# Three memsets ahead of a stage's gathers, and expert slots aligned so that one transfer brings an expert's rows

## The chip, the cores and the metric

The kernel runs on 1 core of one Trainium2 chip, in a single launch. The metric is the device time of that core in microseconds. The engines are TensorE (PE in the profile, with PEld for its weight loads), VectorE (DVE), ScalarE (ACT), GpSimd (POOL) and SyncE (SP). Each runs its own queue of instructions in order and waits on semaphores for the others. GpSimd issues the indirect transfers (gathers and scatters by row index), SP the plain ones.

## What is computed

One block of a graph network over 2500 nodes of 256 features and 80000 edges, in float32. The last two steps are the ones that matter here:

```python
xn = layernorm(x)
x = x + gatv2(xn, edges) + lambda_mix(xn)      # node sums, elu, layernorm, residual
h = layernorm(x)
probs = softmax(h @ gate_w + gate_b)           # 8 experts, top 1
idx, prb = argmax(probs), max(probs)
pos = running count of tokens of the same expert, minus 1
kept = pos < C                                 # C = ceil(1.25 * 2500 / 8) = 391
buf[idx, pos] = h                              # for kept tokens, else dropped
y = relu(buf @ w1 + b1) @ w2 + b2              # per expert, w1 256 x 1024, w2 1024 x 256
x = x + y[idx, pos] * prb * kept               # with nan and inf replaced
```

## The kernel before

Nodes are held as 20 tiles (`TILES`) of 128 nodes, in 5 groups of four tiles (`FOURS`). The kernel has four stages, each a block with one program per engine and a barrier of all engines at its end: `survey` (first layer norm, tables of edges, projections), `attend` (all edges in 176 quads of 512; it leaves running sums in the DRAM array `d_hist`), `node_update`, and `experts`.

**Node update** (lines 1505 to 1819). GpSimd gathers the finished sums of each tile out of `d_hist` into `acc`, one indirect transfer per tile (L1586, 20 in all); the four of group b count up semaphore `fetched[b]`. Behind these it sets three small buffers: `neghalf`, the zero row of `before`, and the padding columns of `pack` (L1588 to L1590). Then it waits for its own memsets and makes reciprocal roots: `roots(b, "var1", ...)` when DVE has `ve1` of group b, and `roots(b - 1, "var2", ...)` when DVE has `ve2`. At last `dispatch(b)` scatters each tile's packed rows to their slots in the DRAM array `d_in` (L1583).

DVE first waits for the memsets (`init` at 2) and writes one column of `pack` (L1644). Then it goes over the groups in a pipeline of five steps, in this order in each round b: `shifts(b-3)`, `logits(b-4)`, `places(b-5)`, `mean_rows(b)` (waits for `fetched[b]`; divides the sums, adds the bias), `residual(b-2)` (needs the first roots and PE's `mix`; writes `x1`), `hidden(b-1)` (elu, adds xn, statistics, writes `ve1`), `choose(b-4)` (the expert of each token). PE runs `mixes(b)` (from the third group on only when `x1` is far enough, as the banks are reused), `turns_of` (transposes and gate products) and `positions` (L1811, L1812: counts in each expert). ACT does exponentials and the second normalization.

SP waits for all five `fetched` semaphores, then loads the weights of experts 0 and 1 (`load_expert`, L1825 to L1828), then stores `x1` of each group to the output.

**Experts** (lines 1831 to 2009). `d_in` holds 391 slots (`CAP`) for each of 8 experts, one behind the other; a row is 516 words (`PACK`): the normalized features, the token's number plus 1, its weight, and `x1`. The slots are cleared in `survey`. `load_rows(e)` brings an expert's slots as four transfers of 98 rows (`CT`), to 98 partitions; the fourth, which is to hold 97, reads one row over into the next expert. Experts 0 to 3 are loaded at the stage's start, one behind the other, expert e + 2 later from the loop over e. PE turns the rows (L1892), widens (L1903), narrows (L1915) and turns back (L1925); ACT empties the banks; DVE cleans the result; GpSimd scatters it to the output.

The order of work is written out by hand for every engine; there is no planner.

Of the kernel before, what the change touches and what calls it, by code (L numbers as in the profile page):

```python
# [26 lines left out]
TILES = -(-NODES // P)  # L27
# [25 lines left out]
EXPERTS, FF = 8, 1024  # L53
CAP = -(-5 * NODES // (4 * EXPERTS))
FCH = FF // P
CT = -(-CAP // 4)
CTS = [CT, CT, CT, CAP - 3 * CT]
TRASH = EXPERTS * CAP
HEAD_COLS = DIM + 4
PACK = HEAD_COLS + DIM  # L60
ZERO_ROWS = 4
# [1443 lines left out]
def node_update(nc, ctx, m, a):  # L1505
# [6 lines left out]
    fetched = [m.sems.enter_context(nc.semaphore(f"upd_fetched{b}")) for b in range(TILES // 4)]  # L1512
    bias, gamma, gate_w, gate_b = m.bias, m.gamma, m.gate_w, m.gate_b
    FOURS = TILES // 4
    acc = sb("u_acc", [P, TILES, HEADS, HCOLS])
    den = sb("u_den", [P, 2, 4 * HEADS])
    out = sb("u_out", [P, 2, 4, DIM])
# [20 lines left out]
    which = sb("u_which", [P, TILES])  # L1538
# [3 lines left out]
    posr = sb("u_posr", [P, TILES])  # L1542
    dropped = sb("u_dropped", [P, TILES])
    at = sb("u_at", [P, TILES])
# [15 lines left out]
    with nc.Block() as block:  # L1560
# [15 lines left out]
        @block.gpsimd  # L1576
        def _(pool):
            def dispatch(b):
                pool.wait_ge(s["packed"], b + 3)
                pool.wait_ge(s["placed"], b + 1)  # L1580
                pool.wait_ge(s["norm"], 4 * b + 4)
                for n in range(4 * b, 4 * b + 4):
                    pool.indirect_dma_start(m.d_in, bass.IndirectOffsetOnAxis(ap=place_all[:, n:n + 1], axis=0),  # L1583
                                            pack[:, n, :], None, bounds_check=TRASH - 1, oob_is_err=False).then_inc(s["scattered"], 16)
            for n in range(TILES):
                pool.indirect_dma_start(acc[:, n, :, :].rearrange("p h c -> p (h c)"), None, m.d_hist,  # L1586
                                        bass.IndirectOffsetOnAxis(ap=m.final[:, n:n + 1], axis=0)).then_inc(fetched[n // 4], 16)
            pool.memset(neghalf[:, :], -0.5).then_inc(s["init"], 1)  # L1588
            pool.memset(before[:, 0:1, :], 0.0).then_inc(s["init"], 1)
            pool.memset(pack[:, :, DIM + 2:HEAD_COLS], 0.0).then_inc(s["packed"], 1)  # L1590
            pool.wait_ge(s["init"], 2)

            def roots(b, var, ve, rs, done):
                cols = slice(4 * b, 4 * b + 4)
                pool.wait_ge(s[var], b + 1)
                rstd_pool(pool, rs[:, cols], ve[:, cols], neghalf[:, :]).then_inc(s[done], 1)
            for b in range(FOURS):
                roots(b, "var1", ve1, rs1, "rstd1")
                if 1 <= b:
                    roots(b - 1, "var2", ve2, rs2, "rstd2")  # L1600
            dispatch(0)
            roots(FOURS - 1, "var2", ve2, rs2, "rstd2")
            for b in range(1, FOURS):
                dispatch(b)
            pool.wait_ge(s["scattered"], 16 * TILES)
# [35 lines left out]
        def _(dve):  # L1641
# [36 lines left out]
            def places(b):  # L1678

                tiles = slice(4 * b, 4 * b + 4)  # L1680
                dve.wait_ge(s["posps"], b + 1)
                ch.step(dve.tensor_tensor(pos[:, tiles, :], ps_pos[:, 4 * b * EXPERTS:(4 * b + 4) * EXPERTS].rearrange("p (n e) -> p n e", n=4),
                                          hot[:, tiles, :], ALU.mult))
                ch.step(dve.tensor_reduce(posr[:, tiles], pos[:, tiles, :], AX.X, ALU.add))
                dve.tensor_scalar(dropped[:, tiles], posr[:, tiles], float(CAP), float(2 * TRASH), ALU.is_gt, ALU.mult).then_inc(s["gate_chain"], 1)
                dve.scalar_tensor_tensor(out=at[:, tiles], in0=which[:, tiles], scalar=float(CAP), in1=posr[:, tiles],
                                         op0=ALU.mult, op1=ALU.add).then_inc(s["gate_chain"], 1)
                dve.scalar_tensor_tensor(out=pack[:, tiles, DIM + 1], in0=posr[:, tiles], scalar=float(CAP), in1=best[:, tiles],
                                         op0=ALU.is_le, op1=ALU.mult).then_inc(s["packed"], 1)
                ch.n += 2  # L1690
                dve.wait_ge(s["gate_chain"], ch.n)
                dve.scalar_tensor_tensor(out=place_all[:, tiles], in0=dropped[:, tiles], scalar=-1.0, in1=at[:, tiles],
                                         op0=ALU.add, op1=ALU.add).then_inc(s["placed"], 1)
# [137 lines left out]
def experts(nc, ctx, m, a):  # L1831
# [5 lines left out]
    rows = [spare[r // 2][:, r % 2, :, :] for r in range(4)]  # L1837
    landed = [m.sems.enter_context(nc.semaphore(f"exp_rows{r}")) for r in range(4)]
# [8 lines left out]
    out = sb("f_out", [P, 2, 4, DIM])  # L1847
# [3 lines left out]
    with nc.Block() as block:  # L1851
        @block.sync
        def _(sp):
            def load_rows(e):
                if e >= 4:
                    sp.wait_ge(s["out"], (e - 3) * 2)
                for j in range(4):
                    lo = e * CAP + j * CT
                    sp.dma_start(rows[e % 4][0:CT, j, :], m.d_in[lo:lo + CT, :]).then_inc(landed[e % 4], 16)  # L1859
            for e in range(4):  # L1860
                load_rows(e)
            for e in range(2, EXPERTS):
                sp.wait_ge(s["y"], (e - 1) * 2)
                load_expert(sp, m, a, e, e % 2)
                if e + 2 < EXPERTS:
                    load_rows(e + 2)
            for q in range(2):
                sp.wait_ge(s["stored"][q], 64 * (EXPERTS // 2))
# [15 lines left out]
        @block.tensor  # L1884
        def _(pe):
            def turn_rows(e):
                pe.wait_ge(landed[e % 4], (e // 4 + 1) * 64)
                if e >= 1:
                    pe.wait_ge(s["rowsb"], e * 2)
                for half in range(2):  # L1890
                    for j, n in enumerate(CTS):
                        last = pe.transpose(m.bank[half][:, j * CT:j * CT + n], rows[e % 4][0:n, j, half * P:half * P + P], m.ident[0:n, 0:n])  # L1892
                    last.then_inc(s["rowst"], 1)
# [67 lines left out]
        def _(dve):  # L1961
            def tokens(e):

                q = e % 2
                dve.wait_ge(landed[e % 4], (e // 4 + 1) * 64)
                if e >= 2:
                    dve.wait_ge(s["stored"][q], e // 2 * 64)
                ids = rows[e % 4][0:CT, :, DIM]
                dve.tensor_scalar(token[0:CT, q, :], ids, 0.0, float(4 * PAD), ALU.is_equal, ALU.mult).then_inc(s["index"], 1)
                dve.wait_ge(s["index"], 2 * e + 1)  # L1970
                dve.scalar_tensor_tensor(out=index[0:CT, q, :], in0=token[0:CT, q, :], scalar=-1.0, in1=ids,
                                         op0=ALU.add, op1=ALU.add).then_inc(s["index"], 1)
# [82 lines left out]
```

## Time and profile before

| | us |
|---|---|
| median of 3 runs | 1382.27 |
| lowest, highest | 1379.01, 1382.58 |
| profiled execution, whole time | 1380.51 |
| its span in the trace | 1378.8 |
| mean granted TensorE clock | 0.924 of full |

The page says that 1138.9 us of the span have PE busy, 1076.6 DVE, 835.5 ACT and 807.0 GpSimd. By stage: the edges take from about 175 to 1033 us, the node update from there to 1167.5, the experts the rest. The time axis of all rows counts from the start of the span. A "busy" share is only what an engine executes; idle time of an engine costs something only where others wait for what it does next.

### The profile page before, as it was taken

How to read it: one execution, taken by the hardware profiler on the slowest of the kernel's cores; microseconds unless marked ns; L12 is line 12 of the kernel's file. 1: busy time of each engine (PE TensorE's matmuls, PEld its weight loads, DVE VectorE, ACT ScalarE, POOL GpSimd, SP SyncE). 2: the span in 40 equal slices, each digit the busy share in tenths (PEclk: the TensorE clock that was granted, in tenths of full speed). 3: DMA queues.
4: the chain of work that ended last, by engine and by line, in shares of the span. 5: the costliest groups of instructions: out<-in, count | busy, mean ns of one | idle time of the engine just before them, and what ended most of it. 6: DMA issues, size and time to landing. Idle time of an engine off the chain costs nothing. (4 is left out here: it accounts for less than half of the span.)

```text
span 1378.8 us, 24446 instructions
## 1 busy us (share of the span) xinstructions
PE 1138.9 (83%) x5685; PEld 838.5 (61%) x5685; DVE 1076.6 (78%) x2310; ACT 835.5 (61%) x3252; POOL 807.0 (59%) x844
## 2 busy tenths in 40 slices
PE   7969789888889989888888989898773553999994
PEld 4537577666667767666666666677552442565652
DVE  5957889998999999899999999999952883044445
ACT  2421278887878888788888887788851231222220
POOL 5217777777777777777777777777805125013133
PEclk9979999999999999999999999999987665899997
DMA  6576578878788888788888877778414313345420
GB/s 167 200 243 187 167 190 208 209 201 198 200 198 207 208 205 202 195 198 206 207 205 208 204 205 189 204 205 210 122 47 135 95 54 138 112 112 150 124 83 16
DMA packets 162621, 234.91 MB, mean 170 GB/s; under 512 B 40085, under 2 KB 131490, under 8 KB 161747
## 3 DMA queue, kind: packets, MB, share of 16 engines
q1 hardware_dynamic: 118434, 127.66, 33.3%
q0 software_dynamic: 41216, 103.67, 29.8%
q10 hardware_dynamic: 2880, 2.66, 0.6%
q14 instruction: 71, 0.58, 0.1%
q8 instruction: 20, 0.33, 0.1%
HBM read 187.01 MB, written 48.91 MB: 171 GB/s over the span
## 5 line engine op out<-in xcount | busy, mean ns | idle before, releaser
L1456 ACT ACTIVATE e_prod<-gathered_rows,e_prod 128x64 f32<-128x64 f32 x2728 | 670.4, 334 | 5.7
L1010 POOL DMA_INDIRECT gathered_rows<-d_xl,e_idx x576 | 549.4, 954 | 175.5 <-issue 163.3
L1400 PE MATMUL bank<-e_prod,e_selt 128*128 128x260 f32 x1408 | 363.7, 404 | 41.7 <-DVE e_acc L1127 21.3
L1400 PEld LDWEIGHTS bank<-e_prod,e_selt 128*128 128x128 f32 x1408 | 273.2, 199 | 96.1 <-issue 46.9
L1346 PE MATMUL bank<-e_xr,e_sel 128*128 128x256 bf16 x2112 | 294.6, 277 | 1.8 <-DVE e_sel L1080 0.4
L1351 PE MATMUL bank<-gathered_rows,ident 128*128 128x256 f32 x704 | 220.6, 395 | 46.5 <-DMA gathered_rows<-d_xl,e_idx 32.5
L1346 PEld LDWEIGHTS bank<-e_xr,e_sel 128*128 128x128 bf16 x2112 | 206.5, 99 | 73.2 <-issue 9.0
L1105 DVE TENSOR_REDUCE e_score<-e_edge 128x16 f32<-128x1024 f32 x176 | 213.0, 1210 | 0.3
L1010 POOL DMA_INDIRECT gathered_rows<-d_xl,src_cols x128 | 122.7, 958 | 71.3 <-issue 36.1
L1351 PEld LDWEIGHTS bank<-gathered_rows,ident 128*128 128x128 f32 x704 | 108.0, 194 | 69.1 <-DMA gathered_rows<-d_xl,e_idx 49.0
L1881 POOL DMA_INDIRECT out_dram<-f_out,f_index x32 | 44.9, 1404 | 160.8 <-DVE f_out L1996 155.9
L1088 DVE TENSOR_TENSOR e_edge<-bank,gathered_rows 128x512 f32<-128x512 f32 x176 | 119.5, 679 | 10.6 <-PE bank L1351 10.4
L1113 DVE TENSOR_TENSOR e_selt<-bank,cyclic_cols 128x512 f32<-128x512 f32 x176 | 119.9, 681 | 0.0
L1094 DVE SCALAR_TENSOR_TENSOR e_edge<-bank,att_relu 128x512 f32<-128x512 f32 x176 | 119.5, 679 | 0.0
L1098 DVE SCALAR_TENSOR_TENSOR e_edge<-e_edge,bank 128x512 f32<-128x512 f32 x176 | 118.6, 674 | 0.0
L1903 PE MATMUL bank<-f_rowst,w_rows 128*128 128x391 f32 x256 | 88.6, 505 | 0.7 <-ACT f_rowst L1944 0.7
L1915 PE MATMUL bank<-f_hid,w_rows 128*128 128x391 f32 x256 | 85.8, 492 | 0.0
L1445 ACT ACTIVATE e_rr<-e_drop 1x4 f32<-1x4 f32 x22 | 4.5, 204 | 125.8 <-DVE e_drop L1185 110.3
L1127 DVE SCALAR_TENSOR_TENSOR e_acc<-e_acc,keep_cols,bank 128x260 f32<-128x260 f32 x154 | 73.2, 475 | 7.3 <-PE bank L1400 7.2
L1903 PEld LDWEIGHTS bank<-f_rowst,w_rows 128*128 128x128 f32 x256 | 49.7, 195 | 38.1 <-issue 3.8
L1951 ACT ACTIVATE f_hid<-bank,b_cols 128x391 f32<-128x391 f32 x64 | 37.6, 588 | 50.6 <-PE bank L1903 50.6
L1915 PEld LDWEIGHTS bank<-f_hid,w_rows 128*128 128x128 f32 x256 | 47.9, 189 | 33.6
(314 smaller groups left out, 1101.1 us busy)
## 6 DMA issues: line engine op xcount, KB each, us to landing
e_xr<-d_xr SPq DMA_DIRECT2D x176, 192.0 KB
d_hist<-e_acc SPq DMA_DIRECT2D x176, 130.0 KB
e_drow<-d_rel SPq DMA_DIRECT2D x176, 128.0 KB
w_rows<-in_L_ffn_w_dram SPq DMA_DIRECT2D x16, 1024.0 KB, 7.2
gathered_rows<-d_xl,e_idx POOLq DMA_INDIRECT x576
d_in<-zero SPq DMA_DIRECT2D x6, 1032.0 KB, 5.0
e_rows<-d_rows SPq DMA_DIRECT2D x22, 192.5 KB
d_xr<-a_xr SPq DMA_DIRECT2D x20, 192.0 KB, 2.0
```

Of the source, the lines that this page charges most:

```text
L1010: pool.indirect_dma_start(xl[:, q.slot * G + g, :], None, m.d_xl, bass.IndirectOffsetOnAxis(ap=column, axis=0)).then_inc(gathered[q.slot], 16)
L1088: dve.tensor_tensor(edge[:, b, 2:4, :], ps_edge[b][1][:, :].rearrange("p (g c) -> p g c", g=2), xl[:, q.slot * G + 2:q.slot * G + 4, 0:DIM ...
L1094: dve.scalar_tensor_tensor(out=edge[:, b, 0:2, :], in0=ps_edge[b][0][:, :].rearrange("p (g c) -> p g c", g=2), scalar=0.0, in1=m.att_relu[ ...
L1098: dve.scalar_tensor_tensor(out=edge[:, b, 2:4, :], in0=edge[:, b, 2:4, :], scalar=0.0, in1=att_relu.unsqueeze(1).to_broadcast([P, 2, DIM]) ...
L1105: dve.tensor_reduce(score[:, p, :, q.at * G:q.at * G + G].rearrange("p h g -> p g h"), edge[:, b, :, :].rearrange("p g (h c) -> p g h c", ...
L1113: dve.tensor_tensor(selt[:, b, :, :], lane_up.unsqueeze(1).to_broadcast([P, G, P]), m.cyclic[:, bass.ds(q.k * G, G)].unsqueeze(2).to_broad ...
L1346: last = pe.matmul(out, sel[:, b, g * P:g * P + P], xr[:, r, part * DIM:part * DIM + DIM], start=(part == 0), stop=(part == 2 and g >= 2))
L1351: last = pe.matmul(out, m.ident[:, :], xl[:, q.slot * G + g, 0:DIM], start=False, stop=True)
L1400: last = pe.matmul(ps_agg[b], selt[:, b, g, :], flat(prod[:, b, g, :, :]), start=(g == 0), stop=(g == G - 1))
L1456: last = act.activation(prod[:, b, g, h, 0:HEAD], xl[:, q.slot * G + g, h * HEAD:h * HEAD + HEAD], ACT.Copy, scale=prod[:, b, g, h, HEAD:H ...
L1903: last = pe.matmul(m.bank[2 + f % 2][:, 0:CAP], w1[:, q, half, f * P:f * P + P], rowst[:, q, half, :], start=(half == 0), stop=(half == 1))
L1915: last = pe.matmul(m.bank[4 + to][:, 0:CAP], w2[:, q, f, to * P:to * P + P], hid[:, f, :], start=(f == 0), stop=(f == FCH - 1))
```

## The change

`node_update`: the three memsets come first in GpSimd's program. Of the 20 gathers, the twelve of groups 0 to 2 follow them; group 3's four are issued behind `roots(0, "var1", ...)`, group 4's behind `roots(1, "var1", ...)` and `roots(0, "var2", ...)`.

`experts`: each expert's slots begin at a multiple of `SLOTS` = 4 x 98 = 392, so slot 391 of every expert is never written and stays zero. One transfer of 98 partitions x 4 rows x 516 words brings an expert's slots in place of four, and the semaphore `landed` counts 16 per expert in place of 64. `TRASH`, the size of `d_in` and the bound of the scatter, grows from 3128 to 3136.

```diff
--- before.py
+++ after.py
@@ -55,7 +55,8 @@
 FCH = FF // P
 CT = -(-CAP // 4)
 CTS = [CT, CT, CT, CAP - 3 * CT]
-TRASH = EXPERTS * CAP
+SLOTS = 4 * CT
+TRASH = EXPERTS * SLOTS
 HEAD_COLS = DIM + 4
 PACK = HEAD_COLS + DIM
 ZERO_ROWS = 4
@@ -1582,12 +1583,15 @@
                 for n in range(4 * b, 4 * b + 4):
                     pool.indirect_dma_start(m.d_in, bass.IndirectOffsetOnAxis(ap=place_all[:, n:n + 1], axis=0),
                                             pack[:, n, :], None, bounds_check=TRASH - 1, oob_is_err=False).then_inc(s["scattered"], 16)
-            for n in range(TILES):
-                pool.indirect_dma_start(acc[:, n, :, :].rearrange("p h c -> p (h c)"), None, m.d_hist,
-                                        bass.IndirectOffsetOnAxis(ap=m.final[:, n:n + 1], axis=0)).then_inc(fetched[n // 4], 16)
             pool.memset(neghalf[:, :], -0.5).then_inc(s["init"], 1)
             pool.memset(before[:, 0:1, :], 0.0).then_inc(s["init"], 1)
             pool.memset(pack[:, :, DIM + 2:HEAD_COLS], 0.0).then_inc(s["packed"], 1)
+            def fetch(b):
+                for n in range(4 * b, 4 * b + 4):
+                    pool.indirect_dma_start(acc[:, n, :, :].rearrange("p h c -> p (h c)"), None, m.d_hist,
+                                            bass.IndirectOffsetOnAxis(ap=m.final[:, n:n + 1], axis=0)).then_inc(fetched[b], 16)
+            for b in range(3):
+                fetch(b)
             pool.wait_ge(s["init"], 2)
 
             def roots(b, var, ve, rs, done):
@@ -1598,6 +1602,8 @@
                 roots(b, "var1", ve1, rs1, "rstd1")
                 if 1 <= b:
                     roots(b - 1, "var2", ve2, rs2, "rstd2")
+                if b + 3 < FOURS:
+                    fetch(b + 3)
             dispatch(0)
             roots(FOURS - 1, "var2", ve2, rs2, "rstd2")
             for b in range(1, FOURS):
@@ -1683,7 +1689,7 @@
                                           hot[:, tiles, :], ALU.mult))
                 ch.step(dve.tensor_reduce(posr[:, tiles], pos[:, tiles, :], AX.X, ALU.add))
                 dve.tensor_scalar(dropped[:, tiles], posr[:, tiles], float(CAP), float(2 * TRASH), ALU.is_gt, ALU.mult).then_inc(s["gate_chain"], 1)
-                dve.scalar_tensor_tensor(out=at[:, tiles], in0=which[:, tiles], scalar=float(CAP), in1=posr[:, tiles],
+                dve.scalar_tensor_tensor(out=at[:, tiles], in0=which[:, tiles], scalar=float(SLOTS), in1=posr[:, tiles],
                                          op0=ALU.mult, op1=ALU.add).then_inc(s["gate_chain"], 1)
                 dve.scalar_tensor_tensor(out=pack[:, tiles, DIM + 1], in0=posr[:, tiles], scalar=float(CAP), in1=best[:, tiles],
                                          op0=ALU.is_le, op1=ALU.mult).then_inc(s["packed"], 1)
@@ -1854,9 +1860,7 @@
             def load_rows(e):
                 if e >= 4:
                     sp.wait_ge(s["out"], (e - 3) * 2)
-                for j in range(4):
-                    lo = e * CAP + j * CT
-                    sp.dma_start(rows[e % 4][0:CT, j, :], m.d_in[lo:lo + CT, :]).then_inc(landed[e % 4], 16)
+                sp.dma_start(rows[e % 4][0:CT, :, :], m.d_in[e * SLOTS:(e + 1) * SLOTS, :].rearrange("(j p) c -> p j c", p=CT)).then_inc(landed[e % 4], 16)
             for e in range(4):
                 load_rows(e)
             for e in range(2, EXPERTS):
@@ -1884,7 +1888,7 @@
         @block.tensor
         def _(pe):
             def turn_rows(e):
-                pe.wait_ge(landed[e % 4], (e // 4 + 1) * 64)
+                pe.wait_ge(landed[e % 4], (e // 4 + 1) * 16)
                 if e >= 1:
                     pe.wait_ge(s["rowsb"], e * 2)
                 for half in range(2):
@@ -1962,7 +1966,7 @@
             def tokens(e):
 
                 q = e % 2
-                dve.wait_ge(landed[e % 4], (e // 4 + 1) * 64)
+                dve.wait_ge(landed[e % 4], (e // 4 + 1) * 16)
                 if e >= 2:
                     dve.wait_ge(s["stored"][q], e // 2 * 64)
                 ids = rows[e % 4][0:CT, :, DIM]
```

## Rows read from the trace of the kernel before

**Rows 1.** Page, part 1: each engine's busy time, share of the span, and instructions.
```profile
PE 1138.9 (83%) x5685; PEld 838.5 (61%) x5685; DVE 1076.6 (78%) x2310; ACT 835.5 (61%) x3252; POOL 807.0 (59%) x844
```

**Rows 2.** Windows by stage: busy time of each engine, granted clock, DMA share, GB/s.
```profile
core 0: us, PE busy (x) PEld busy (x) DVE busy (x) ACT busy (x) POOL busy (x), PEclk, DMA share, GB/s
175.00:1020.00 845.00, 740.81 (x4131) 571.80 (x4129) 783.77 (x1521) 693.37 (x2912) 626.94 (x650) 0.97 0.77 195
1020.00:1150.00 130.00, 72.26 (x294) 59.67 (x293) 81.04 (x258) 36.50 (x91) 40.20 (x44) 0.69 0.30 99
```

**Rows 3.** Waits of DVE, 1030 to 1175: total us, times, longest.
```profile
DVE u_pack L1644 <- POOL u_before L1589: 28.2, 1, 28.2
...
DVE u_pos L1682 <- PE bank L1812: 6.7, 5, 4.5
```

**Rows 4.** Timeline of POOL, node update: start, duration, what, idle before it and releaser.
```profile
1035.26 0.96 POOL L1586 DMA_INDIRECT u_acc<-d_hist,final_rows  x1 [37.13 <-POOLq L953]
...
1039.03 0.95 POOL L1586 DMA_INDIRECT u_acc<-d_hist,final_rows  x1 [0.30 <-issue]
...
1059.94 0.13 POOL L1588 MEMSET u_neghalf<- 128x4 f32 x1
...
1060.02 0.16 POOL L1590 MEMSET u_pack<- 128x40 f32 x1
1070.64 1.04 POOL L232 TENSOR_TENSOR u_rs<-u_ve,u_neghalf 128x4 f32<-128x4 f32 x1 [10.46 <-DVE u_ve L1725]
```

**Rows 5.** The tile u_acc: its 20 gathers, from issue to landing.
```profile
DMA to landing us min/median/max: 2.6/2.8/3.7
```

**Rows 6.** Timeline of DVE, node update.
```profile
1060.30 0.17 DVE L1700 TENSOR_SCALAR u_den<-u_acc 128x16 f32<-128x16 f32 x1
...
1063.19 0.17 DVE L1700 TENSOR_SCALAR u_den<-u_acc 128x16 f32<-128x16 f32 x1
...
1070.32 0.17 DVE L1725 TENSOR_SCALAR u_ve<-u_mv 128x4 f32<-128x4 f32 x1
...
1082.46 0.17 DVE L1725 TENSOR_SCALAR u_ve<-u_mv 128x4 f32<-128x4 f32 x1
...
1084.81 0.17 DVE L1700 TENSOR_SCALAR u_den<-u_acc 128x16 f32<-128x16 f32 x1
...
1096.87 0.17 DVE L1725 TENSOR_SCALAR u_ve<-u_mv 128x4 f32<-128x4 f32 x1
...
1156.38 0.16 DVE L1692 SCALAR_TENSOR_TENSOR u_place_all<-u_dropped,u_at 128x4 int32<-128x4 f32 x1
```

**Rows 7.** The chain that ended last, first pieces of the expert stage: start, us, what.
```profile
1167.60 0.34 SPq L1859
...
1168.68 0.38 SPq L1859
...
1169.10 4.09 DMA xn_rows<-d_in
...
1175.53 13.76 PE bank L1903 x32
...
1200.54 10.53 PE bank L1903 x32
```

**Rows 8.** Timeline of SP: the first weight transfer.
```profile
1061.77 0.41 SPq L1825 DMA_DIRECT2D w_rows<-in_L_ffn_w_dram  x1
```

**Rows 9.** Groups of POOL by line: busy us, mean ns, idle before and releasers.
```profile
L1010 POOL DMA_INDIRECT gathered_rows<-d_xl,e_idx x576 | 549.4, 954 | 175.5 <-issue 163.3 <-ACT e_prod L1456 12.2
...
L1881 POOL DMA_INDIRECT out_dram<-f_out,f_index x32 | 44.9, 1404 | 160.8 <-DVE f_out L1996 155.9 <-issue 4.9
```

**Rows 10.** Timeline of PE, the fifth group's `mixes` and what follows them.
```profile
1111.45 2.05 PE L1780 MATMUL bank<-w_mix,xnt_rows 128*128 128x256 f32 x4
...
1116.71 1.04 PE L1780 MATMUL bank<-w_mix,xnt_rows 128*128 128x256 f32 x4
...
1119.31 0.30 PE L1811 MATMUL bank<-u_hot,tri 128*128 128x32 f32 x2
```

**Rows 11.** Window of one us in which row transfers of the expert stage run (columns as in rows 2).
```profile
1176.00:1177.00 1.00, 1.00 (x3) 0.37 (x3) 0.34 (x2) 0.00 (x0) 0.00 (x0) 0.50 0.94 301
```

## The prediction

> **What bounds the kernel now.** I read the page's head first: VectorE (DVE) and TensorE (PE) are both about 80% busy over the span, which settles nothing, because it is a mean over stages [rows 1]. The stretch of the node update, 1020 to 1150 us, looks different: PE 72 of 130 us, DVE 81, GpSimd (POOL) 40, DMA share 0.30 [rows 2]. Nothing is full there, so the stage is bound by a chain, and the question is where it starts and what it waits for.
>
> The waits of DVE in that stage name one large stall: 28.2 us in front of the first DVE instruction of the stage, released by POOL's memset of `u_before` at L1589 [rows 3]. The timeline of POOL shows why it is long: POOL issues 20 gathers one behind the other from 1035.26, one every 1.25 us, and reaches its memsets only at 1059.94 [rows 4]. The gathers themselves land 2.6 to 3.7 us, median 2.8, after their issue [rows 5]. The fourth gather, issued at 1039.03, has landed by 1041.8, and with it the data of the first four tiles; DVE starts on them at 1060.30 [rows 4 to 6]. So for 18.5 us DVE has its data and waits for 0.3 us of memsets behind 16 more gathers.
>
> Who is late because of it: all that follows hangs on DVE's own products. POOL's first root waits from 1060.18 to 1070.64 for `u_ve` [rows 4], which DVE finishes at 1070.49 [rows 6]; PE turns to the third group of tiles when `x1` comes. The stage ends with POOL's scatters to `d_in`, which need what DVE writes last, at 1156.38 [rows 6]; then SyncE (SP) begins the expert stage at 1167.60, in which the chain runs on PE's matmuls to near the end [rows 7]. A shift of DVE's start is a shift of the end unless something in between is tied to the clock time and not to DVE.
>
> **The memsets and the order of the gathers.** Cost on POOL: three memsets of 0.24 us in all (1059.94 to 1060.18 [rows 4]) now stand in front of the first gather. I put the gathers 0.3 us later: first 1035.55, fourth 1039.3, eighth 1044.3, twelfth 1049.3, last of the three groups done at about 1050.5. This follows the rows of before, 1.25 us apiece.
>
> DVE's first group: data at 1039.3 + 2.8 = 1042.1 against 1060.30, 18.2 us earlier. Second group: DVE takes 2.9 us for a group's means (1060.30 to 1063.19 [rows 6]) and would be free at 1045.0, but the eighth gather lands only at 1044.3 + 2.8 = 1047.1. The second group thus begins 1063.19 - 1047.1 = 16.1 us earlier, not 18.2, and what follows it in DVE's order (the first group's `hidden`) comes after it. **16.1 us is the gain of this part.** `u_ve` of group 0 is then ready at 1070.49 - 16.1 = 1054.4.
>
> Now what is moved behind the roots. POOL ends its twelve gathers at 1050.5 and waits for 1054.4: the first root costs nothing extra. It then issues group 3's four gathers, 5.0 us, from 1055.7 to 1060.7. Its next root needs the next `u_ve` of DVE, at 1082.63 - 16.1 = 1066.5 [rows 6]: 5.8 us of cover. Group 3 has landed by 1062.4 and DVE asks for it at 1084.81 - 16.1 = 1068.7 [rows 6]. Group 4's gathers go out between about 1068.7 and 1073.7, behind two roots; the next root has its input at 1097.04 - 16.1 = 1080.9 [rows 6], and DVE asks for group 4 only after it has made that, against a landing near 1075.5. If this cover were gone, each group of four would cost up to 5 us.
>
> SP's queue: it waits for all five groups before it loads two experts' weights. That moves from 1061.77 [rows 8] to about 1075.5, 14 us later, with the stores of `x1` behind it. The weights' first reader is PE at 1175.53 [rows 7], which becomes 1159, more than 80 us after the issue; I cost it at nothing.
>
> What could widen or shrink the 16.1: the landing of the eighth gather at 2.6 or 3.7 us instead of 2.8 gives +0.2 or -0.9. The last gathers of the eight now run beside DVE's first group. In the message stage, where DVE is 93% busy (783.77 of 845 us [rows 2]), 576 gathers averaged 954 ns against 944 here with DVE idle; the nearest dear row is the experts' scatters, other in shape, at 1404 ns [rows 4, 9]. I take the former, being the same operation; the latter on three gathers would cost 3 x 0.46 = 1.4 us. The Trainium skill (SBUF — State Buffer, "SBUF: two separate sides") warns of just this overlap: while DVE runs a two-port operation, GpSimd can't write descriptors, and a transfer of some 620 ns took about 3100. By that figure, as an estimate, the change would lose, see rival C; the 954 ns beside a busy DVE do not agree with it here [rows 9].
>
> TensorE's clock: the stage has stretches at the low level (0.50, or 1.2 GHz) and at full. One place touches the path: DVE waits 4.46 us of the 6.7 in [rows 3] for PE's L1812, behind four tiles of `mixes` that took 7.86 us, 1111.45 to 1119.31, two at the low level (5.26, 1111.45 to 1116.71) and two at full (2.60) [rows 10]. PE does the same work in the same order after the change, so I cost it at zero; all four at full would give 2.6 us, all at low would cost 2.7. The first expert's widening took 13.76 us against 10.53 of the later ones [rows 7]: up to 3.2 us less, or about as much more, if the rise comes elsewhere. I take none of it.
>
> **The aligned slots and the single transfer.** Removed: three of four SP issues per expert, 24 in all; `d_in` gets 8 more rows, cleared by a slightly longer last store in the survey, nothing. For experts 4 to 7 the rows land long before PE asks, and the chain shows PE back to back [rows 7]. Only expert 0 is on the path: issues begin at 1167.60, the fourth at 1168.68, and PE waits for that one's landing, 4.09 us from 1169.10 [rows 7]. With one transfer the last issue is the first: at most 1168.68 - 1167.60 = 1.1 us saved. But an expert's 392 rows of 516 words, 0.81 MB, at the 301 GB/s of [rows 11] need 2.7 us of transfer anyway, partly done before the fourth issue. I take **0.5 us**, between -0.5 (one transfer starts slower than four in a row) and 1.1.
>
> **Sum.** 16.1 + 0.5 = 16.6 us. The profiled execution took 1380.51 us for a span of 1378.8, so it would give 1363.9. It lies between the timed ones (1379.01, 1382.27, 1382.58); the mean of the four is 1381.1, and 1381.1 - 16.6 = **1364.5 us**.
>
> **Rivals.**
> A, *fewer DMA engines for the one transfer* (partly given back). The four transfers of before were in flight together. If the single one were spread by its piece index (4) and not by its 98 rows, 4 engines would carry it: 301 x 4/16 = 75 GB/s, 0.81 MB in 10.8 us in place of 2.7, so PE starts 8.1 us later, less the 1.1 of issue. Expert 1, queued behind, lands another 10.8 us on, before PE asks for it behind the 13.76 us of widening. Gain 16.1 - 7.0 = 9.1, time 1372.0. Speaking for: the pattern does gain a middle dimension; against: partitions stay outermost on both sides. The Trainium skill (DMA: Bandwidth & Descriptors, "Why a DMA increments its semaphore by 16 and not by 1") says that the largest divisor up to 16 of the slowest dimension sets the number of engines; by it 98 gives 14 before and after, and no change.
>
> B, *the stage does not follow DVE* (no change). If a thing tied to the clock time sets the end, the DVE shift is hidden and only the 0.5 us stay: about 1380.5. Candidates are SP's weights and stores, 14 us later than now. Against it: they have the 80 us of cover above, and each stall in the waits has DVE, PE or POOL work derived from DVE as its releaser [rows 3].
>
> C, *gathers starve beside a busy DVE* (slower). Twelve gathers now stand ahead of the first root. With g us per gather the root starts at 1035.5 + 12g; before it started at 1070.64 [rows 4]. That meets at g = 2.9 us, against 1.25 now. Above it the kernel loses: at g = 3.5 the first root is at 1077.5, 6.9 late; group 3's gathers then end at 1092.5 where the next root has its input at 1089.5, 3.0 more; group 4's cost about 1.6 more: +11.5 us, 1392.6. It decides only where DVE works, and the rows above give 1.25 to 1.7.
>
> **How the numbers follow.** Forecast 0.87, A 0.06, B 0.03, C 0.03, and 0.01 for a gain past all bounds. All bounds at once give 16.6 - 0.9 - 1.4 - 2.7 - 3.2 - 1.0 = 7.4 and 16.6 + 0.2 + 2.6 + 3.2 + 0.6 = 23.2; they will not all fall one way, so I take about half of each side, and 1.5 us for the spread of the runs shown: 1359 to 1371. It leaves out most of A, and B and C. About 0.3%, 4 us, is what a measurement tells from no change. Faster: forecast, A and the large gain, 0.94; same: B, 0.03; slower: C, 0.03.
>
> **What would show it.** DVE's first instruction of the stage near 1035 and its first means near 1042; the second group's means near 1047, with a short wait on the gathers in between; gathers of 0.95 us throughout, in groups of 12, 4 and 4; roots without waits on POOL itself; SP's weights near 1075; the end of the stage near 1151.5 instead of 1167.6; one row transfer per expert, PE at it about 5.2 us after SP begins, against 5.7. The forecast is wrong if a wait of more than 2 us on gathers or roots appears behind group 1, if gathers last over 1.5 us, or if PE starts the first expert later than 6.5 us after SP.

## The result, and the profile after

The changed kernel takes 1370.85 us (median of 4 runs, 1370.56 to 1371.12). The kernel before, beside it, takes 1380.64 us (4 runs, 1378.71 to 1382.58). The ratio is 0.9929, interval [0.9911, 0.9947]: 9.8 us faster, where 16.6 were forecast. Ratios, here and below, leave out the slow runs that a kernel can have; medians and ranges are over all runs. The profiled execution of after took 1370.74 us for a span of 1368.8, at a mean granted clock of 0.926, against 1378.8 at 0.924.

The page's head, as [rows 1], tells as little as it did before; all busy times are within 2 us of theirs:

```profile
PE 1137.2 (83%) x5685; PEld 839.9 (61%) x5685; DVE 1078.4 (79%) x2310; ACT 835.6 (61%) x3252; POOL 807.8 (59%) x844
```

So I cut both spans at points that both kernels have. "End of survey" is the time from the end of SP's last issue there (the store of `links`) to its first issue in the edge stage (`e_drow`). "Node update" is from PE's first `mixes` to SP's first issue of the expert stage.

| stretch | before, us | after, us | difference |
|---|---|---|---|
| up to the end of SP's last survey issue | 90.32 | 92.30 | +1.98 |
| end of survey | 6.21 | 11.14 | +4.93 |
| edges | 938.1 | 936.7 | -1.4 |
| node update | 132.99 | 116.86 | -16.13 |
| experts, to the end | 211.20 | 211.84 | +0.64 |
| sum | 1378.8 | 1368.8 | -10.0 |

The node update gave what was forecast. Some of the gain was lost in a stage 900 us earlier, at a step that the prediction had put at nothing.

**Node update.** Timeline of POOL in after: start, duration, what, idle before it and releaser. It answers [rows 4].

```profile
1040.06 0.10 POOL L1586 MEMSET u_neghalf<- 128x4 f32 x1 [35.25 <-POOLq L954]
...
1040.84 0.97 POOL L1591 DMA_INDIRECT u_acc<-d_hist,final_rows  x1 [0.56 <-issue]
...
1049.61 1.03 POOL L1591 DMA_INDIRECT u_acc<-d_hist,final_rows  x1 [0.30 <-issue]
...
1053.45 1.63 POOL L1591 DMA_INDIRECT u_acc<-d_hist,final_rows  x1 [0.30 <-issue]
...
1060.00 1.04 POOL L233 TENSOR_TENSOR u_rs<-u_ve,u_neghalf 128x4 f32<-128x4 f32 x1 [3.66 <-DVE u_ve L1731]
...
1072.08 2.03 POOL L233 TENSOR_TENSOR u_rs<-u_ve,u_neghalf 128x4 f32<-128x4 f32 x2 [5.70 <-DVE u_ve L1731]
```

The memsets now start at the head. The first root still waits for `u_ve` (3.66 us), and so does the pair of roots behind group 3's gathers (5.70 us): twelve gathers ahead of the first root, and the fourth group's four (`b` = 3, "group 3" below) ahead of the next, delay none of them. Timeline of DVE in after, which answers [rows 6]:

```profile
1040.31 0.18 DVE L1650 TENSOR_SCALAR u_pack<-tile_ids 128x20 f32<-128x20 f32 x1 [2.62 <-POOL u_before L1587]
1048.10 0.17 DVE L1706 TENSOR_SCALAR u_den<-u_acc 128x16 f32<-128x16 f32 x1 [7.60 <-DMA u_acc<-d_hist,final_rows]
...
1052.54 0.17 DVE L1706 TENSOR_SCALAR u_den<-u_acc 128x16 f32<-128x16 f32 x1 [1.46 <-DMA u_acc<-d_hist,final_rows]
1053.04 1.23 DVE L1712 TENSOR_TENSOR u_out<-u_acc,u_den 128x1024 f32<-128x1024 f32 x1
...
1059.67 0.17 DVE L1731 TENSOR_SCALAR u_ve<-u_mv 128x4 f32<-128x4 f32 x1
...
1145.76 0.16 DVE L1698 SCALAR_TENSOR_TENSOR u_place_all<-u_dropped,u_at 128x4 int32<-128x4 f32 x1
```

The 28.2 us of [rows 3] have become 2.62 on the memsets, 7.60 on the first group's landing and 1.46 on the second's. The stage began 5.49 us later than before (1040.10 against 1034.61, the loss at the survey's end among it), so times have to be read from its start: the second group's means begin at 12.44 us instead of 28.58, **16.14 us earlier**, and the stage is 16.13 us shorter. The first group alone came 17.7 us earlier, but the landing behind it took 1.5 of these.

**Experts.** SP's and PE's timelines of after; before, PE had its first rows at 1173.33, 5.73 us after SP began at 1167.60 [rows 7].

```profile
1156.96 1.05 SPq L1863 DMA_DIRECT2D xn_rows<-d_in  x2
```

```profile
1162.88 1.54 PE L1896 MATMUL bank<-ident,xn_rows 98*128 98x98 f32 x8 [17.87 <-DMA xn_rows<-d_in]
```

With a single transfer it takes 5.92 us, so this span shows no saving.

**End of survey.** SP's timeline before and after, from its last store to `d_in` on:

```profile
86.60 0.43 SPq L377 DMA_DIRECT2D d_in<-zero  x1
...
89.05 1.27 SPq L395 DMA_DIRECT2D links<-n_links_t  x1
...
96.53 0.34 SPq L964 DMA_DIRECT2D e_drow<-d_rel  x1
```

```profile
88.49 0.28 SPq L378 DMA_DIRECT2D d_in<-zero  x1
...
90.29 2.01 SPq L396 DMA_DIRECT2D links<-n_links_t  x1
...
103.44 0.35 SPq L965 DMA_DIRECT2D e_drow<-d_rel  x1
```

From the start of the last clearing store to the first `e_drow` it is 9.93 us before and 14.95 after. What the chip does in that time is shown by one window of after (columns as in [rows 2]):

```profile
95.00:101.00 6.00, 0.00 (x0) 0.00 (x0) 0.00 (x0) 0.00 (x0) 0.00 (x0) 0.50 0.06 21
```

No engine works for 6 us, and the DMA share is 0.06, which is one of 16 engines, moving 21 GB/s. The waits of SP from 85 to 105 us say what it stands at, before and then after:

```profile
SPq L397 <- DMA d_xr<-a_xr: 3.8, 1, 3.8
```

```profile
SPq L398 <- DMA d_xr<-a_xr: 8.7, 1, 8.7
```

By name this is the last store of `d_xr`, which SP issued behind the clearing store and which is the same before and after; its wait is 4.9 us longer. That it had to queue behind the clearing store on the engine that carries it fits the rows, but is argued. The experiments below show that the clearing store is what makes the difference.

### The profile page after: what moved, and what is told of

It is laid out like the page before. It is cut to its first block and busy times, and to the rows that moved or that the text cites. A ratio compares the mean times of both kernels' runs of the same rounds, so it can differ in the third digit from the quotient of the medians.

```text
span 1368.8 us, 24422 instructions
## 1 busy us (share of the span) xinstructions
PE 1137.2 (83%) x5685; PEld 839.9 (61%) x5685; DVE 1078.4 (79%) x2310; ACT 835.6 (61%) x3252; POOL 807.8 (59%) x844
```

## Experiments

**How their times are read.** The experiments ran on three chips; that of the result isn't named, but I take it for another, since the edge stage takes 1275 to 1340 us in the experiments instead of 937, in every kernel. Why, the traces don't say: in e2, DVE waits there 227 us ahead of `e_edge` for a releaser that isn't named. Single whole times are 1699 to 1780 us, and those of one kernel scatter by 20 or more in most cases. The stages outside it are about as long as here, so I read the experiments by the stages above, from one profiled span of each kernel, and give the whole time only where it says something. Four kernels ran beside each other on the first of these chips (e1 to e4), four on the second (e1b, e5 to e7), two on the third (e8, e9).

| kernel | partitions of the last clearing store | its issue to first `e_drow` | end of survey | node update | experts |
|---|---|---|---|---|---|
| before | 15 | 9.93 | 6.21 | 132.99 | 211.20 |
| after | 17 | 14.95 | 11.14 | 116.86 | 211.84 |
| e1 | 16 | 9.80 | 6.09 | 119.48 | 210.34 |
| e2 | 17 | 14.95 | 11.18 | 133.82 | 210.02 |
| e3 | 15 | 9.66 | 5.91 | 119.64 | 210.75 |
| e4 | 15 | 9.86 | 6.13 | 122.69 | 210.45 |
| e1b | 16 | 10.13 | 6.43 | 119.71 | 210.34 |
| e5 | 16 | 10.25 | 6.54 | 119.66 | 210.10 |
| e6 | 34 of 2 rows | 11.53 | 8.05 | 119.00 | 210.16 |
| e7 | 16 | 10.19 | 6.48 | 119.64 | 211.53 |
| e8 (after again) | 17 | 14.97 | 11.17 | 119.79 | 210.16 |
| e9 (e1 again) | 16 | 9.85 | 6.12 | 118.20 | 209.91 |

**What makes the end of the survey longer.** The theory: `TRASH` grew by 8 rows, so `blank` = `TRASH` + 4 grew from 3132 to 3140, and the last clearing store, four rows to a partition, grew from 15 partitions to 17; 17 is prime, and one DMA engine moves it all. The rivals: the order of the node update shifts something earlier, or it is the scatter of the chip. e1 takes the 17 partitions away from the changed kernel (the four rows behind `TRASH`, which nobody reads, stay uncleared) and e1b does the same on another chip; e2 gives it to the kernel before.

```diff
-            blank = TRASH + ZERO_ROWS
+            blank = TRASH
```

> The changed kernel, but the survey clears exactly the 3136 slots: the last clearing transfer then covers 64 rows on 16 partitions instead of 68 rows on 17. Theory N (narrow clearing): the changed kernel lost about 5 us of its gain at the end of the survey, because the 17-partition transfer moves at 23 to 25 GB/s (DMA share 0.07) from 94 to 101 us and the barrier waits for it. Then this kernel takes about 1370.85 - 5.0 = 1365.9 us, and the survey's last SP issue is followed by the first of the edge stage within about 6 us instead of 11. Rival E (early loads and chance): the late start of the edge stage comes from the first loads or from scatter between programs, and the last clear has nothing to do with it: 1370.9, with the gap still at 11 us.

> The same kernel as e1 once more (the changed kernel with the last clearing transfer on 16 partitions), since the earlier comparison ran where the edge stage alone differed by tens of microseconds from run to run. Theory N: gap from the survey's last SP issue to the first of the edge stage about 6.1 us as in e1, against 11.1 in the changed kernel; whole time 1365.9 where the kernel before takes 1380.6. Rival E: gap 6.1 but time not below the changed kernel's 1370.9, something else having taken the 5 us.

```diff
-            blank = TRASH + ZERO_ROWS
+            blank = TRASH + 3 * ZERO_ROWS
-    m.d_in = dram("d_in", (TRASH + ZERO_ROWS, PACK))
+    m.d_in = dram("d_in", (TRASH + 3 * ZERO_ROWS, PACK))
```

> The kernel before, with nothing changed but the clearing of the slots: 3140 rows are cleared instead of 3132 (the array is 8 rows longer), so the last clearing transfer has 68 rows on 17 partitions instead of 60 rows on 15. Theory N: about 5 us slower than before, 1380.6 + 5.0 = 1385.6, and low DMA rates of some 24 GB/s for about 7 us ahead of the barrier. Rival E: no difference from before, 1380.6.

Measured: with 16 partitions the changed kernel's end of survey is 6.09 and 6.43 us; with 17 the kernel before has 11.18. SP's timeline of e1, then of e2:

```profile
87.69 0.42 SPq L378 DMA_DIRECT2D d_in<-zero  x1
...
90.12 1.28 SPq L396 DMA_DIRECT2D links<-n_links_t  x1
...
97.49 0.35 SPq L965 DMA_DIRECT2D e_drow<-d_rel  x1
```

```profile
87.60 0.28 SPq L377 DMA_DIRECT2D d_in<-zero  x1
...
89.40 1.97 SPq L395 DMA_DIRECT2D links<-n_links_t  x1
...
102.55 0.34 SPq L964 DMA_DIRECT2D e_drow<-d_rel  x1
```

The 5 us go with the 17 partitions and with nothing else of the change. The whole time doesn't resolve them on these chips: e2 has 1750.87 us beside 1747.28 of before, ratio 1.0112 [0.9886, 1.0339], and e1 1750.37, both of them with runs up to 1769 and more; for e1 there is no ratio. e1b, on the second chip, took 1710.86 us, ratio 0.9867 [0.98, 0.9933].

Is it the number of engines or the 8 more rows? e6 keeps the changed kernel's bytes and makes 34 partitions of two rows of them; 34 is divisible by 2, so two engines should move it.

```diff
             def blank_slots(lo):
                 n = min(P * ZERO_ROWS, blank - lo) // ZERO_ROWS
+                if n == 17:
+                    sp.dma_start(m.d_in[lo:lo + 68, :].rearrange("(p r) c -> p r c", r=2),
+                                 m.zero[0:34, 0:2, :]).then_inc(m.prepared, 16)
+                    return
```

> The changed kernel with its last clearing transfer of 68 rows laid out as 34 partitions of 2 rows instead of 17 of 4. The same bytes. The Trainium skill (DMA: Bandwidth & Descriptors, Why a DMA increments its semaphore by 16 and not by 1) says the largest divisor up to 16 of the slowest dimension sets the number of DMA engines, 1 for 17 and 2 for 34. Theory K (number of engines by divisor): the low tail of DMA traffic moves at twice the rate, some 48 GB/s and share 0.12, and ends 3 to 3.5 us earlier, gap about 7.5 to 8 us instead of 11.1. Rival B (the bytes or the late issue are what counts): gap still 11.

Window of e6 (columns as in [rows 2]):

```profile
94.00:96.00 2.00, 0.00 (x0) 0.00 (x0) 0.00 (x0) 0.00 (x0) 0.00 (x0) 0.50 0.13 48
```

Twice the share (0.13) and twice the rate (48 GB/s), and the end of the survey at 8.05 us, in between. The same bytes on two engines cost 3.1 us less than on one. That settles the number of engines as the cause. (The whole time of e6 is 1712.07 us, ratio 0.9887 [0.9813, 0.9961].) By size: the store is 68 rows of 516 words, 140 thousand bytes (the 137.1 KB of the profile, at 1024), and the window of 6 us at 21 GB/s holds 126 thousand of them. The whole of it takes 140 / 21 = 6.7 us at that rate and 140 / 48 = 2.9 us at e6's, 3.8 us less, where 3.1 were measured. Before, 120.9 KB landed 3.4 us after their issue. The Trainium skill (DMA: Bandwidth & Descriptors, "Why a DMA increments its semaphore by 16 and not by 1") gives the rule, the largest divisor up to 16 of the slowest dimension: 15 for 15, 16 for 16, 1 for 17, 2 for 34. The windows of 17 and 34 agree with it (shares of 1/16 and 2/16); of 15 and 16 the rows show only that both are short and alike.

**What the two halves of the node update's change are worth.** e3 is the kernel before with the new order of gathers and memsets alone (no aligned slots, no single transfer). e4 only moves the three memsets ahead of all 20 gathers.

```diff
+            pool.memset(neghalf[:, :], -0.5).then_inc(s["init"], 1)
+            pool.memset(before[:, 0:1, :], 0.0).then_inc(s["init"], 1)
+            pool.memset(pack[:, :, DIM + 2:HEAD_COLS], 0.0).then_inc(s["packed"], 1)
             for n in range(TILES):
                 pool.indirect_dma_start(acc[:, n, :, :].rearrange("p h c -> p (h c)"), None, m.d_hist,
                                         bass.IndirectOffsetOnAxis(ap=m.final[:, n:n + 1], axis=0)).then_inc(fetched[n // 4], 16)
-            pool.memset(neghalf[:, :], -0.5).then_inc(s["init"], 1)
-            pool.memset(before[:, 0:1, :], 0.0).then_inc(s["init"], 1)
-            pool.memset(pack[:, :, DIM + 2:HEAD_COLS], 0.0).then_inc(s["packed"], 1)
```

> The kernel before with the memsets and the new order of the gathers alone; the slots, their clearing and the four row transfers per expert are those of before. The sum of the prediction: the node update ends 16.1 us earlier, 1380.6 - 16.1 = 1364.5. Theory N expects just that, as the survey is untouched: edge stage starting where it starts in the kernel before. Rival O: the late start belongs to the changed order in some way (the program's layout, for instance), and this kernel ends near the changed one, 1370.9.

> The kernel before with the three memsets first, but all 20 gathers in one row behind them, ahead of the first root. By the rows of the changed kernel: the gathers would end 25 us after the first, 20 us after group 0 lands; the first root would come about 6 us later than in the changed kernel, of which DVE can cover 3.2 us with the third group's means and the gamma products. So the memsets are worth about 13.3 us and the split of the gathers about 2.8: 1380.6 - 13.3 = 1367.3. Rival: the order of the gathers behind the memsets gives nothing (DVE has enough other work), 1364.5, equal to the kernel with the order alone.

On that chip the old order takes 133.82 us (e2), memsets first 122.69, and the full order 119.64: 11.1 us for the memsets, 3.05 for putting the roots between the gathers. The second was expected at 2.8, the first at 13.3 (more on this below). That is where the first root's wait shows in e4, in DVE's waits between 1380 and 1560 us (total us, times, longest):

```profile
DVE u_pack L1739 <- POOL u_rs L232: 3.2, 1, 3.2
```

and in its POOL timeline, the last gather and the root right behind it, with no idle time between:

```profile
1435.67 0.95 POOL L1589 DMA_INDIRECT u_acc<-d_hist,final_rows  x1 [0.30 <-issue]
1436.64 1.04 POOL L232 TENSOR_TENSOR u_rs<-u_ve,u_neghalf 128x4 f32<-128x4 f32 x1
```

In e3 that wait is absent. e3's whole time is 1730.71 us beside 1747.28, ratio 0.9957 [0.9847, 1.0067], and e4's is 1741.19, ratio 1.0043 [0.9955, 1.0131]; neither can be told from no change.

On this chip the full order is worth 14.2 us, and 16.1 on the first one. The rows of e2 and e3 account for the 1.9 between. About 0.4 is the second group's landing: its means begin 28.61 us after the stage's start in e2 (1428.07) and 12.85 after it in e3 (1422.86), 15.76 earlier and not 16.14, since a gather ahead of that landing took longer (see the last section). Another 1.4 is DVE's wait on PE's counts, 3.27 us in e2 and 4.67 in e3. PE did the same work ahead of it at another clock. The turns and gate products of the tiles ahead of the fifth group's `mixes` took 4.94 us in e2 (from 1470.44) at a mean granted clock of 0.83, and 5.86 in e3 (from 1465.38) at 0.64; the `mixes` themselves took 7.60 and 8.06. One group of gate products in e2, at the higher clock, and the same one in e3, at the lower:

```profile
1472.27 0.58 PE L1787 MATMUL bank<-gate_w,u_normt 128*128 128x8 f32 x4 [0.90 <-ACT u_normt L1626]
```

```profile
1467.20 0.99 PE L1792 MATMUL bank<-gate_w,u_normt 128*128 128x8 f32 x4 [0.89 <-ACT u_normt L1631]
```

e4 has the long wait too (4.4 us), which is 1.1 of the 2.2 us by which the memsets fell short of 13.3. DVE also waits 5.5 us ahead of `u_lg` on this chip against 3.2 on the first, but it does so in e2, e3 and e4 alike, so no difference between them comes of it; why it is longer there I did not isolate.

**One transfer or four.** e5 is e1 with four row transfers per expert again (the two waits on `landed`, not shown, count to 64 again).

```diff
-                sp.dma_start(rows[e % 4][0:CT, :, :], m.d_in[e * SLOTS:(e + 1) * SLOTS, :].rearrange("(j p) c -> p j c", p=CT)).then_inc(landed[e % 4], 16)
+                for j in range(4):
+                    lo = e * SLOTS + j * CT
+                    sp.dma_start(rows[e % 4][0:CT, j, :], m.d_in[lo:lo + CT, :]).then_inc(landed[e % 4], 16)
```

> As e1b, but every expert's rows are again brought by four transfers of 98 rows, from the aligned slots. This sets the single transfer's worth apart. The prediction said 0.5 us in its favour. The traces of before and after say against: PE began 5.73 us after the expert stage's first issue before (1167.60 to 1173.33) and 5.92 after (1156.96 to 1162.88). Theory S (bound by the transfer itself, 0.81 MB): the two kernels agree within 0.3 us, with PE's first transpose 5.7 to 5.9 us after the first issue in both. Rival of the prediction: the single transfer is 0.5 us or more faster.

From SP's first issue of the stage to PE's first transpose, e5 has 5.87 us (1497.10 to 1502.97) and e1b, beside it, 5.93 (1534.36 to 1540.29). First SP, then PE, of e5:

```profile
1497.10 3.24 SPq L1865 DMA_DIRECT2D xn_rows<-d_in  x7
```

```profile
1502.97 1.54 PE L1898 MATMUL bank<-ident,xn_rows 98*128 98x98 f32 x8 [17.83 <-DMA xn_rows<-d_in]
```

Over all kernels: four transfers 5.73, 5.69, 5.87, 6.11, 6.07 (before, e2, e5, e3, e4; mean 5.89), one transfer 5.92, 5.93, 5.84, 5.79, 5.96, 5.82, 5.75 (after, e1b, e1, e6, e7, e8, e9; mean 5.86). There is no difference to be seen, and the whole times agree: e5 1712.01 us, ratio 0.9887 [0.9846, 0.9927], e1b 1710.86.

**A try at the experts' tail.** DVE seemed to reach the last expert's results late because it handles the next expert's tokens first. e7 is e1 with DVE taking `results(e - 1, ...)` ahead of `tokens(e)`.

```diff
             for e in range(EXPERTS):
-                tokens(e)
                 if e >= 1:
                     results(e - 1, 0)
                     results(e - 1, 1)
+                tokens(e)
```

> As e1b, and in the expert stage DVE makes the next expert's index (which waits for the landing of a scatter, up to 12 us behind the weight transfers) after the results of the expert before, no longer ahead of them. In the traces DVE reaches the last expert's results 1.35 us after PE's last product in the kernel before, and 2.2 us in the changed one, where it is still busy with the expert before. Theory T: the expert stage gets shorter by 0.6 to 0.8 us, 1365.2 in all. Rival: nothing moves, since GpSimd's scatters then wait for the later index.

There was no gain: the experts take 211.53 us, against 210.34, 210.10 and 210.16 on the same chip, and the whole time is 1717.69 us, ratio 0.993 [0.9886, 0.9974]. DVE reaches the last results 0.68 us after PE begins to turn them back (1684.09). But so it does without this edit on the same chip (0.68 to 0.77 us in e1b, e5 and e6) and in before (0.69); only the span of after has 1.36. So there was nothing left to gain here. The loss is one operation of DVE, which takes four times as long as the same operation behind it, 1.3 us more. DVE's timeline of e7, then POOL's at that time:

```profile
1686.11 1.73 DVE L1989 TENSOR_SCALAR f_bad<-f_ys 98x512 int32<-98x512 f32 x1
...
1687.76 0.41 DVE L1990 TENSOR_SCALAR f_bad<-f_ys 98x512 int32<-98x512 f32 x1
```

```profile
1685.42 2.16 POOL L1885 DMA_INDIRECT out_dram<-f_out,f_index  x1 [0.30 <-issue]
```

The slow one lies beside a scatter's issue and ends 0.26 us after it. That the scatter holds it up fits the rows but is argued, not shown. The scatter itself isn't slowed: the kernel's last one takes the same 2.16 us, at 1698.97, with DVE idle.

**After, and the repaired version, side by side.** e8 is the changed kernel as it is, e9 is e1 again.

> The changed kernel itself, beside the one below and the kernel before on the same chip. Both theories: survey gap 11.1 us, node update 117 to 120 us. It anchors the pair: theory N wants it about 5 us behind the kernel below, rival E level with it.

> The changed kernel with the last clearing transfer on 16 partitions, again, on the same chip as the changed kernel. Theory N: 5 us less than the run above, in whole time as in the gap between the survey's last SP issue and the edge stage's first (6.1 to 6.4 against 11.1). Rival E: gap shorter, whole time level.

By stages it repeats: the end of the survey is 11.17 us in e8 and 6.12 in e9. Whole times: e8 1717.76 us (1701.93 to 1741.33), ratio to before 0.9885 [0.983, 0.9941]; e9 1710.54 (1699.73 to 1722.08), ratio 0.9871 [0.9821, 0.9922]. The two ratios differ by 0.0014, some 2.4 us in e9's favour, and their intervals overlap widely. Both are faster than before; that e9 beats the changed kernel is shown in its stage and not in the whole time. Taking its 5.0 us off the 1370.85 gives an estimate of 1365.9 us on the first chip, where it wasn't run.

## Why the prediction was right and wrong

**Right: the main term.** 16.1 us were forecast for the node update and 16.13 measured. The step that decided it held too: the gain is set by the second group's landing and not by the first's. The second group's means were forecast 16.1 us earlier, and came 16.14 earlier. The first group's were forecast 18.2 earlier and came 17.7, its last gather having taken 3.5 us to land instead of the 2.8. A forecast that had stopped at the stall of 28.2 us, or at the 18.2 us of the first group, would have been too high.

**Right: the cover behind the roots.** 5.8 us of cover were forecast for group 3's gathers; the idle time that is left before the pair of roots is 5.70. SP's first weight transfer was forecast at 1075.5 and came at 1081.12, which is the same place in a stage that began 5.5 us later. It cost nothing. e4 prices what the split saves, 3.05 us.

**Wrong: the step "`d_in` gets 8 more rows, cleared by a slightly longer last store in the survey, nothing".** It cost 4.93 us, half of what the whole change brought. The mistake was to price the store by its bytes (120.9 to 137.1 KB) and not to write down its shape. 3140 rows in stores of 128 x 4 leave 68, and 68 / 4 = 17 partitions. The prediction had the rule on DMA engines at hand and applied it to the 98 rows, where the change left the number as it was; it did not apply it to the one transfer whose partitions the change altered. Nor did it ask who waits for that store: a barrier of all engines.

**Luck.** The measured 1370.85 us lies inside the stated range, 1359 to 1371, by 0.15 us. The range held it by luck: its slow side was made of a late landing, slow gathers, TensorE's clock and a slower single transfer, and these took almost nothing. What used it up is the clearing store, which had been put at nothing.

**Wrong in size: the single transfer.** 0.5 us forecast, 0.03 measured as the difference of the means (5.89 less 5.86), within the bounds of -0.5 to 1.1 and less than the kernels differ among themselves. The term that failed was the saving of 1.1 us of issues, of which half was to be left. Windows of one us, the second of the stage before and then in after (columns as in [rows 2]):

```profile
1168.60:1169.60 1.00, 0.00 (x0) 0.00 (x0) 0.00 (x0) 0.00 (x0) 0.48 (x2) 0.50 0.77 208
```

```profile
1158.00:1159.00 1.00, 0.00 (x0) 0.00 (x0) 0.00 (x0) 0.00 (x0) 0.44 (x1) 0.50 0.63 109
```

With four transfers the first ones are moving while the fourth is issued, and in this second window they move twice as much. After it the single transfer moves faster (336 and 326 GB/s against 239 and 211) and draws level. That it shares the engines with expert 1's rows, whose single transfer after issues within the first 1.05 us as well, may cost it part of this; no run takes that apart.

**The rest.** Of the 6.6 us between the forecast gain and the measured difference of the spans (16.6 less 10.0), 4.93 are the end of the survey and 1.14 the experts (0.5 expected and missed, 0.64 longer). The remaining 0.5 is the survey's 1.98 more, against the 1.4 less of the edges and 0.03. In the experiments the store of `d_in` that lies at 86.60 before and at 88.49 after starts anywhere from 86.93 to 88.52, in no order that follows the code (87.60 in e2, 87.14 in e8), so I take the 1.98 for scatter. The 0.64 of the experts has a place in the rows: in after DVE reaches the last expert's results 1.36 us after PE begins to turn them back, being still at work on the expert before, and 0.69 after it in before. I take that for scatter too, since e8, the same kernel, has 0.68.

**The rivals.** A, fewer DMA engines for the row transfer, forecast PE 8.1 us later less 1.1; PE started 0.2 us later, so it is false, but its mechanism struck at another transfer. B is false: the stage followed DVE to within 0.02 us. C is false: the twelve gathers ahead of the first root took 1.29 us apiece with the gaps between them (1040.84 to 1056.34), far from the 2.9 us at which it would decide. The prediction's witness against C, the mean of 954 ns in the edge stage, was weaker than it sounds: no row says whether the operations that keep DVE busy there are of the two-port kind that it names.

**The signs.** Two of the signs that were to show the forecast wrong came, and meant nothing. One gather lasted over 1.5 us (1.63, at 1053.45), but POOL had 3.66 us to spare behind it. And behind group 1 DVE waits twice for over 2 us on roots (2.15 and 2.16 us), but it waited for them before as well (2.10 and 2.09): a sign has to be set against the same row of before. PE's start on the experts, forecast at 5.2 us, missed.

**Clock.** Costed at zero. DVE's total wait on the counts of PE is 6.6 us against 6.7 [rows 3], and the first expert's widening took 13.63 us against 13.76; it stayed near zero on the path. It need not have: between e2 and e3 the same wait on the counts grew by 1.4 us with PE's clock, inside the 2.7 us that the prediction allowed.

## What to carry to other kernels

When a change alters an array's size, follow that size to every loop that tiles it, and write the shape of the last, partial transfer before and after; ask what its outer dimension is divisible by and which barrier waits for it. When a stall is removed from a pipeline, take the gain from the second item's arrival and not the first's. And issue time that merging transfers removes isn't time saved as long as the earlier ones are moving: here 1.1 us of issues gave nothing that could be measured.

## What was unexpected of the hardware

A single DMA engine moved 21 GB/s in after and two moved 48 in e6, writing rows of 516 words from SBUF to DRAM. The issue of the 17-partition store is shorter on SP than that of the 15 or 16 (0.28 against 0.42 us), although its landing is so much later, and so is that of e6's 34 (0.28): the issue time says nothing of the cost. The `links` store that follows it is issued in 2.01 us instead of 1.27.

A gather whose issue begins while DVE runs the 1.23 us product `u_out` <- `u_acc`, `u_den` (two inputs and an output in SBUF) ended 0.81 to 0.83 us after that product, however early it began, and 0.90 after it where it came straight behind a root. In after the product at 1053.04 ends at 1054.27, and the gather at 1053.45 ends at 1055.08; the one at 1049.61 ends at 1050.64, 0.81 after the product of 1048.60. e3's rows, DVE first, then POOL:

```profile
1417.71 1.23 DVE L1711 TENSOR_TENSOR u_out<-u_acc,u_den 128x1024 f32<-128x1024 f32 x1
...
1422.86 0.17 DVE L1705 TENSOR_SCALAR u_den<-u_acc 128x16 f32<-128x16 f32 x1 [2.67 <-DMA u_acc<-d_hist,final_rows]
```

```profile
1418.29 1.46 POOL L1590 DMA_INDIRECT u_acc<-d_hist,final_rows  x1 [0.30 <-issue]
```

1417.71 + 1.23 + 0.81 = 1419.75 = 1418.29 + 1.46. e4 has the same gather beside the same product, to 0.02 us. So such a gather is held back, by at most 0.7 us, which a mean of 954 ns over 576 gathers [rows 9] hides. The Trainium skill (SBUF — State Buffer, "Who interferes with whom") infers that such an operation of DVE doesn't hold up descriptor generation; these rows speak against it for a gather's issue as a whole, by tenths of a microsecond. But the same section of the Trainium skill says that a DVE instruction with two SBUF inputs contends with a GpSimd instruction that reads SBUF, and a gather reads its row numbers from there; whether that read or the descriptors were held up, the rows don't tell. In after it cost about 0.1 us on the path, in e3 about 0.5, both inside the 1.4 us that the prediction had bounded it with.
